# Schur and solve steps for two chunks at once, key, value and query products in one-bank halves, and another rule for the order of the steps

## Reference, cut to what matters

```python
def step(S, qkv):                       # scanned over the 8 chunks of a batch, for each head
    Qc, Kc, Vc = qkv                    # 128 x 64 each
    G = Kc.T @ Kc + 1e-4 * I
    W = jnp.linalg.solve(G, Kc.T @ Vc)
    U = I[:, :8]
    for _ in range(2):
        U, _ = jnp.linalg.qr(W @ U)
    Wr = U @ (U.T @ W)
    S_new = 0.9 * S + Wr
    return S_new, 0.125 * (Qc @ S_new)
```

## Time and profile before

| | |
|---|---|
| median of 3 runs | 1141.81 us (1141.43 to 1143.41) |
| the profiled execution | 1141.08 us |
| its span in the trace | 1139.3 us |
| busy: PE, DVE, ACT, POOL | 976.5, 650.0, 536.2, 196.8 us |
| mean granted clock of TensorE | 0.916 of 2.4 GHz |
| DMA | 117.49 MB, mean 103 GB/s |

### The profile page before, as it was taken

One profiled execution on the slowest core, in us unless ns is written; L12 is line 12 of the kernel. 1 busy time (PEld: TensorE's weight loads), 2 busy tenths in 40 slices (PEclk: granted clock), 3 DMA queues, 4 the chain that ended last, 5 costly groups with the idle time before them and its releaser, 6 DMA issues.

```text
span 1139.3 us, 41225 instructions
## 1 busy us (share of the span) xinstructions
PE 976.5 (86%) x18210; PEld 732.9 (64%) x18210; DVE 650.0 (57%) x1439; ACT 536.2 (47%) x1064; POOL 196.8 (17%) x246
## 2 busy tenths in 40 slices
PE   4898898996889986567988899899578989999997
PEld 2454445653545555446877788687456878888886
DVE  5772980999669995153675676588321243333333
ACT  2653334633544554342545544356444544444445
POOL 3431000010020001000122132221000232222223
PEclk9999999998999996677998999899656999999999
DMA  9543126634664576443144321423444121111100
GB/s 289 165 142 93 56 88 155 168 120 109 169 170 96 155 187 183 101 109 88 51 139 126 98 66 41 118 64 93 133 101 103 56 53 40 40 41 40 40 20 20
DMA packets 210912, 117.49 MB, mean 103 GB/s; under 512 B 145776, under 2 KB 197360, under 8 KB 209712
## 3 DMA queue, kind: packets, MB, share of 16 engines
q1 hardware_dynamic: 205264, 93.62, 31.3%
q0 software_dynamic: 5472, 21.24, 6.1%
HBM read 61.74 MB, written 53.08 MB: 101 GB/s over the span
## 4 chain that ended last, share of the span: by engine, by line
PE 73%; DMA 7%; ACT 7%; issue 5%; SPq 4%; DVE 4%; POOL 1%; POOLq 0%; DVEq 0%; ACTq 0%
PE psum L1107 19%; PE psum L1295 10%; PE psum L1117 9%; PE psum L1127 5%; PE psum L1328 5%; PE psum L1318 5%; PE psum L1214 3%; PE psum L1284 3%; DMA cu<-gc_d 3%; DMA schur_mem<-lead_d 2%; PE psum L1271 2%; PE psum L1200 2%; PE psum L1180 2%; ACT kv L740 2%; PE psum L1155 2%
## 5 line engine op out<-in xcount | busy, mean ns | idle before, releaser
L1107 PE MATMUL psum<-wqkv,xhat 128*128 128x512 f32 x512 | 241.0, 621 | 2.5 <-ACT xhat L732 2.3
L968 DVE SCALAR_TENSOR_TENSOR outer<-sweep_mem,rd 128x992 f32<-128x992 f32 (+30 forms) x248 | 187.4, 755 | 8.7
L974 DVE TENSOR_TENSOR sweep_mem<-sweep_mem,outer 128x992 f32<-128x992 f32 (+30 forms) x248 | 177.7, 716 | 8.5
L1107 PEld LDWEIGHTS psum<-wqkv,xhat 128*128 128x128 f32 x512 | 97.2, 197 | 115.5 <-issue 112.8
L740 ACT COPY kv<-psum 128x1024 f32<-128x1024 f32 x64 | 64.8, 1012 | 164.7 <-PE psum L1107 164.7
L1295 PE MATMUL psum<-wo,kv 128*128 128x256 f32 x512 | 124.4, 398 | 0.7 <-DVE state L1027 0.4
L1117 PE MATMUL psum<-xhat,wqkv 128*128 128x128 f32 x1024 | 124.6, 281 | 0.3 <-ACT nz L829 0.3
L669 POOL TENSOR_TENSOR hsplit<-gc,hsplit 128x512 f16<-128x512 f32 x64 | 74.6, 1166 | 284.9 <-ACT hsplit L860 284.8
L1117 PEld LDWEIGHTS psum<-xhat,wqkv 128*128 128x128 f32 x1024 | 120.6, 197 | 2.0 <-ACT nz L829 0.4
L1295 PEld LDWEIGHTS psum<-wo,kv 128*128 128x128 f32 x512 | 98.5, 197 | 16.1 <-DVE state L1027 0.6
L855 ACT ACTIVATE gc<-psum,b1c,alpha 128x128 f32<-128x128 f32 x256 | 96.8, 468 | 19.1 <-PE psum L1318 19.1
(11 more groups left out here) (117 smaller groups left out, 1389.0 us busy)
## 6 DMA issues: line engine op xcount, KB each, us to landing
gc_d<-gc SPq DMA_DIRECT2D x32, 512.0 KB, 3.4
schur_mem<-gc_d SPq DMA_DIRECT2D x32, 384.0 KB, 3.9
f_d<-fac SPq DMA_DIRECT2D x32, 272.0 KB, 2.2
fl<-f_d SPq DMA_DIRECT2D x32, 272.0 KB, 2.9
sv_d<-sv SPq DMA_DIRECT2D x32, 192.0 KB, 2.8
lead_d<-sweep_mem POOLq DMA_DIRECT2D x4, 1024.0 KB, 5.1
schur_mem<-lead_d SPq DMA_DIRECT2D x64, 64.0 KB, 3.7
r_d<-pt SPq DMA_DIRECT2D x32, 128.0 KB, 2.0
```

The source lines that it names most:

```text
L968: V.scalar_tensor_tensor(out=tile, in0=a[:, t, t + 1:HALF].unsqueeze(2).broadcast_to([P, m, HALF]), scalar=rd[:, t:t + 1], in1=a[:, t, t + ...
L974: V.tensor_tensor(rest, rest, tile, ALU.subtract).then_inc(swept, 1)
L1107: ins = mm(dst[:, cols], xnt[:, c, t], wqkv[:, n, t, cols], start=t == 0, stop=t == KT - 1)
```

## The change

`side()` is now called after every host step and tries one Schur step and one solve step. Both chains work on a pair of chunks (`e`, chunks 2e and 2e + 1), one pair at a time; a step is put only when the plan takes its predecessor's drain or load to be done (`ready`). `K`, `V` and `Q` become `KA`, `KB`, `VA`, `VB`, `QA`, `QB` of one bank and one ACT copy each. `WRA` and `WRB` of a turn come behind `QA` and `QB` of that same turn (one turn of the loop earlier). The plan's weights are new, DVE may be 1.2 us behind PE when a pivot is put, and banks are chosen by another key. The alternate buffers now hold the two chunks of a pair, so all but `gct` (still two pairs) are single for a pair. `NZ`'s results are read with another index (`2 * b + n`), with the same instructions.

```diff
-SIDE_EVERY = 1.7
+DVE_BEHIND = 1.2
-            if start > now["pe"]:
+            if start > now["pe"] + DVE_BEHIND:
                 return
+    def ready(step, c):
+        return max([0.0] + [at.get(e, 1e9) for e in follows(step, c)])
+    def bank(n):
+        def key(k):
+            t = max(free[k:k + n])
+            beside = max(free[k ^ 1], now["pe"]) if n == 1 else 0.0
+            return max(t, now["pe"]), -beside, k
+        return min(range(0, NBANKS, n), key=key)
...
-    def schur_slot():
...
+    def load_schur():
+        e = chain["schur_next"]
+        if e < NCH // 2 and at.get(("swept", 0, e // half_batch), 1e9) <= now["pe"]:
+            put("LC", e)
+            chain["schur"] += [("SP", e), ("SX", e), ("SV", e)]
+            chain["schur_next"] += 1
+    def schur_step():
+        if not chain["schur"]:
+            load_schur()
+        if not chain["schur"] or ready(*chain["schur"][0]) > now["pe"]:
+            return False
+        step, e = chain["schur"].pop(0)
+        put(step, e)
+        if step == "SP":
+            load_schur()
+        elif step == "SV" and e % half_batch == half_batch - 1:
+            open_at[1, e // half_batch] = at["SV", e] + 4.0
+        return True
+    def load_solve():
+        e = chain["solve_next"]
+        if e < NCH // 2 and at.get(("swept", 1, e // half_batch), 1e9) <= now["pe"]:
+            put("LS", e)
+            chain["solve"] += [("S", e), ("U", e), ("W", 2 * e), ("W", 2 * e + 1), ("Y", e), ("YT", e), ("Z", e)]
+            chain["solve_next"] += 1
+    def solve_step():        # as schur_step; the two W are put together, then load_solve(); after the batch's last Z, MLOAD
...
     def side():
-        return schur_slot() or solve_slot()
+        done = [schur_step(), solve_step()]
+        return any(done)
     def host(step, c):
         put(step, c)
-        main[0] += PE_WEIGHT.get(step, 0.0)
-        if main[0] >= SIDE_EVERY:
-            main[0] = 0.0
-            side()
+        side()
...
-        for step, at in (("K", c), ("V", c), ("T", c + 1), ("G", c)):
+        for step, e in (("KA", c), ("KB", c), ("VA", c), ("VB", c), ("T", c + 1), ("G", c)):
...
-        if on(r + 1):
-            put("WRA", r + 1)
-            put("WRB", r + 1)
...
         if on(r + 2):
-            host("Q", r + 2)
+            host("QA", r + 2)
+            host("QB", r + 2)
+            put("WRA", r + 2)
         if on(r):
             host("Y3", r)
+        if on(r + 2):
+            put("WRB", r + 2)
```

SP's load of a pair for the solve steps, and an ACT drain and a matmul step as examples of the rest:

```diff
-            def load_solve(c):
+            def load_solve(e):
...
-                if c >= 2:
-                    sp.wait_ge(*is_filled("U", c - 2))
+                if e:
+                    sp.wait_ge(*is_filled("U", e - 1))
+                for i in range(2):
+                    sp.dma_start(lps[:, i], comp_d[b].rearrange("(s c q) t n -> c (q t) s n", c=CPB, q=QUADS)[c % CPB + i]
+                                 ).then_inc(solve_loaded, 16)
+                    sp.dma_start(vv[:, i], sv_d[c + i][:, :, HALF:]).then_inc(solve_loaded, 16)
-                if c >= 2:
-                    sp.wait_ge(*is_filled("W", c - 2))
+                if e:
+                    sp.wait_ge(*is_filled("W", c - 1))
...
+                for a in range(2):
+                    for u in range(2):
+                        sp.dma_start(cu[rows(2 * a), u], src[rows(2 * a), u, :, :, HD:P]).then_inc(solve_loaded, 16)
...
+            def lower_rows(e):
+                act.wait_ge(*is_filled("U", e))
+                if e:
+                    act.wait_ge(*is_filled("W", 2 * e - 1))
                 for a in range(2):
                     sl = rows(2 * a + 1)
-                    ins = nc.scalar.copy(cu[sl, c % 2].rearrange("p (s u) n -> p u s n", u=2), src[sl])
-                ins.then_inc(drain("U", c), 1)
+                    ins = nc.scalar.copy(cu[sl].rearrange("p u c s n -> p (u c s n)"), place("U", e)[sl])
+                ins.then_inc(drain("U", e), 1)
...
             def gram(c):
                 dst = begin("G", c)
-                pe.wait_ge(*is_drained("K", c))
-                pe.wait_ge(*is_drained("V", c))
-                for h in range(PAIRS):
+                for half in range(2):
+                    pe.wait_ge(*is_drained(("KA", "KB")[half], c))
+                    pe.wait_ge(*is_drained(("VA", "VB")[half], c))
+                    for h in range(4 * half, 4 * half + 4):
```

More of the change, by code:

```diff
@@ new lines, in load_solve @@
+    def load_solve():
[5 more added lines that the diff above has]
+    def solve_step():
+        if not chain["solve"]:
+            load_solve()
+        if not chain["solve"] or ready(*chain["solve"][0]) > now["pe"]:
+            return False
+        step, e = chain["solve"].pop(0)
+        put(step, e)
+        if step == "W":
+            if e % 2 == 0:
+                put(*chain["solve"].pop(0))
+            load_solve()
+        elif step == "Z" and e % half_batch == half_batch - 1:
+            put("MLOAD", e // half_batch)
+            small_at[e // half_batch] = now["pe"] + 7.0
@@ L227, in load_factors @@
     def load_factors(r):
-        if 0 <= r < turns and r not in factors and ("Z", TURNS[r]) in where:
+        if 0 <= r < turns and r not in factors and ("Z", TURNS[r] // 2) in where:
             put("LF", r)
@@ new lines, in comp_inverse @@
+            def comp_inverse(e):
+                dst = begin("S", e)
+                pe.wait_ge(solve_loaded, 160 * (e + 1))
+                for c in range(2):
+                    for s in range(PAIRS // 2):
+                        at = HALF * (PAIRS // 2 * c + s)
+                        for q in range(QUADS):
+                            sl = rows(q)
+                            ins = mm(dst[sl, at:at + HALF], lps[sl, c, s, HALF:], lps[sl, c, s, 0:HALF], start=True, stop=True)
+                ins.then_inc(fill("S", e), 1)
@@ new lines, in lower_rows @@
+            def lower_rows(e):
+                dst = begin("U", e)
+                pe.wait_ge(*is_drained("S", e))
+                for c in range(2):
+                    for s in range(PAIRS // 2):
+                        for q in range(QUADS):
+                            at = BANK * (q % 2) + HD * (PAIRS // 2 * c + s)
+                            ins = mm(dst[rows(q | 1), at:at + HD], st[rows(q), c, s], vv[rows(q), c, s], start=True, stop=True)
+                ins.then_inc(fill("U", e), 1)
```

494 lines of the change are left out of this document (230 added, 264 removed).

## The result

The changed kernel takes 1045.3 us (median of 4 runs, 1041.37 to 1051.75) against 1141.62 (4 runs, 1139.5 to 1143.41): ratio 0.916, 95% interval 0.911 to 0.922. It is 96 us faster where 153 were forecast. The time lies in the range (950 to 1050) and near its slow end; it is outside the likeliest case's own range (955 to 1015). The profiled execution took 1048.18 us with a span of 1046.3 and a clock of 0.949.

What follows compares the result with a forecast made beforehand. PE bounds the kernel, busy 86% of the span, with two stretches of side steps only (174.5 us). Terms 413 + 5 + 295.5 + 3 + 282 = 998.5, less 12 for loads, give 986.5, so 988 us; range 950 to 1050.

Steps and rivals of the forecast that it cites:

- the likeliest case: Both stretches without host steps, before the first turn and before batch 2, all but closed: 955 to 1015 us, chance 0.62.
- loads covered: DMA waits for S and SP outside the two stretches, about 23 us: host steps between load and use take 12 off.
- Four pairs after a load of 6 us: 293 + 6 + 88 = 387: Batch 0's solve chain in the first stage: sweep 3 ends at 293, load 6 us, four pairs of 22 us.
- batch 0 can be there at 411: Batch 0's inverses before the first turn: small inverse and its way back add 24 us to the solve chain's end at 387.
- Rival 1: Solve loads late: all 16 pairs wait on PE, up to 59 us where 33 is paid now; 1014 us, chance 0.10.
- Part 1: Halves of K, V, Q: G's 17.8 us wait for V's copy goes (10 to 17.8), for 18 us of hidden ACT time.
- Part 2: WRA and WRB one turn earlier, no longer in front of WO: 13 us gained, bounds 0 and 18.
- Part 3, first stage: More side calls: first stage ends at 413 with 4 further solve chunks; wait before first turn falls from 101.5 to 5 us.
- Part 3, turns: Turns up to batch 2 take 295.5 us with 16 solve, 12 Schur chunks; sweeps take 80 us, batch 2 there at 681.
- The wait of 73 us goes to 0: PE's stretch without host steps before batch 2: batch 2 there at 681, before 713.5; 3 us left in the sum.
- rival 3: Batch 0 late, at 483: readiness test passes a pair only in 40 us; 70 us of waiting, about 1055 us, chance 0.07.
- rivals 1 and 2: First: late solve loads, 1014 us, chance 0.10. Second: sweeps among turns stay at 116 us, batch 2 late, about 1030, chance 0.13.

Runs made afterwards that it cites:

- parts 1 and 2 alone: The kernel before with halves of K, V, Q and WRA and WRB one turn earlier, old side slots kept: 1120.09 us, ratio 0.985.
- batch 2 held: The changed kernel with the solve chain tried first and Schur steps of batches 2 and 3 held until batch 0's last Z is put: 1035.25 us, ratio 0.908.
- the combined kernel: The changed kernel with batch 2 held and batch 0's small inverse moved behind the last pivot of sweep 5: 1030.72 us, ratio 0.906.

## Why the prediction was right in sign and short in size

The stretches, forecast and found:

| part of the sum | forecast | found | off |
|---|---|---|---|
| first stage, to last G | 413 | 429.1 | + 16 |
| wait before the first turn | 5 | 34.6 | + 30 |
| turns up to batch 2, with its wait | 298.5 | 314.3 | + 16 |
| rest | 282 | 268.3 | - 14 |
| loads covered | - 12 | in the parts above | + 12 |
| span | 986.5 | 1046.3 | + 60 |

**The step that failed** is "Four pairs after a load of 6 us: 293 + 6 + 88 = 387", with what is built on it, "batch 0 can be there at 411". The first NZ was possible at 463.7. By its terms: sweep 3 ended at 302.1 and not 293 (+ 9; the sweep before it started at 192.8 after 196.5, only 4 us earlier), from there to the first S were 27.4 us and not 6 (+ 21), the four pairs took 329.5 to 431.0 = 101.5 and not 88 (+ 14), and from Z to the first NZ went 32.7 and not 24 (+ 9). The biggest of these was readable before: the path from sweep 3 to the first S was 35.5 us in the kernel before (305.9 to 341.4). The 6 us is the constant that the plan uses for it, and I took the plan's figure where the trace had one. The Trainium skill (DMA: Bandwidth & Descriptors, Rules for kernel authors) wants a DMA issued early; the rows above show that here the issue itself was late, for 12 us behind a store in the same queue. Rival 1 looked for this loss 16 times over, as a wait of PE on each load (up to 59 us, found 1.6); it came once, on the path, and no row of PE's waits shows it, because PE did host work meanwhile.

**Part 1** was right in its mechanism (17.8 us of waits gone, and ACT's price as reckoned: 556.0 us busy with parts 1 and 2 alone after 536.2, + 20 where 18 was counted; in the changed kernel the drains of a pair save more than that, 531.4) and too small for this kernel, by what the halves do for the side steps: some 33 us by the run with whole K, V and Q.

**Part 2** was put at 13, between 0 and 18; measured some 7 to 10 by ratios, with intervals that overlap or nearly touch.

**Part 3, first stage.** The + 16 has two halves. PE's idle time in it fell from 52.1 to 43.3, by 9, where 17.8 was counted; new waits of small steps took the rest. And its busy time rose by 19.4 instead of 12.4. I had kept "no extra" for the clock, with the argument that the small matmuls now lie between long ones. They do, and the clock is still lower: 0.95 in the first stage, against 0.98. The window of the changed kernel in which the side steps are thickest, and PE's timeline around its start:

```profile
391.00:408.00 17.00, 15.07 (x362) 10.04 (x362) 15.75 (x37) 5.82 (x11) 0.00 (x0) 0.63 0.44 124
```

```profile
385.30 1.88 PE L1134 MATMUL psum<-wqkv,xhat 128*128 128x512 f32 x4
391.16 2.10 PE L1186 MATMUL psum<-schur_mem 32*32 32x32 f32 x64 [3.99 <-DMA schur_mem<-lead_d]
...
394.31 3.14 PE L1134 MATMUL psum<-wqkv,xhat 128*128 128x512 f32 x4
```

PE is busy for 15.07 of 17 us there, and the clock is 0.63. But the window begins behind a wait: PE stood idle for 3.99 us for the load of a Schur pair, and in it the clock fell to 0.50 (at 390). It rose, and fell again at 400, when PE had stood idle once more, for 1.8 us. At the low level the long products are slow as well, four in 3.14 us where they took 1.88 just before, and small steps directly behind long ones have the full clock: 64 matmuls of 32 x 32 take 1.20 us at 429.0. In the first stages of this kernel and of the one before, each of the ten falls of the clock comes in or directly behind an idle time of PE, of 1.3 to 7.6 us. So the small matmuls by themselves are not what lowers the clock here; the falls go with the waits that the side steps bring. With batches 2 and 3 held back these waits are gone from the end of the stage. The same window of the changed kernel and of the one with batch 2 held:

```profile
330.00:402.00 72.00, 64.15 (x1589) 40.44 (x1578) 67.67 (x127) 36.05 (x60) 0.84 (x3) 0.94 0.58 143
```

```profile
330.00:402.00 72.00, 68.72 (x1668) 42.43 (x1667) 67.71 (x126) 41.41 (x66) 0.85 (x3) 1.00 0.45 121
```

The clock is 1.00 instead of 0.94, PE is busy 4.6 us longer, and the last G comes at 409.1 (402.6 to 411.2 in the four kernels that hold batch 2). So part of the extra time is the price of Schur work that was put there before it was needed: its waits, and the clock that they cost.

**Part 3, turns.** "The wait of 73 us goes to 0" is right: 0, not even the 3 I left. But sweep 6 could not start at 403 as the sum has it; it is batch 3's first sweep and needs the last G. It started at 457.0, behind the small inverse of batch 0. The 80 us for a sweep among the turns held for the sixth (79.9) and not for the seventh (107.4), so that sweep 7 ended at 644.2, not 563. Batch 2 came in time all the same, the loads of its inverses issued by 773.7 and used by NZ at 789.1 with no wait, so at most 15 us of the forecast's margin of 32 are left. How thin that is the experiments show: two small edits of the order (the load planned 8 us earlier, DVE not allowed behind) bring the stretch back with 42 and 50 us. The turns up to batch 2 took 39 us more than before, where 27 less 6.5 was forecast, plus 3 for a wait. The matmuls in the windows say why: these turns held 7 to 8 solve chunks before, not the 10 that the sum starts from, and hold 18 to 20 now, not 16; the Schur chunks stayed 8 and did not become 12 (4 lie in the wait of 34.6 us). PE's busy time there rose by 35 us and its idle time by 4. The rest is 14 shorter than forecast because it holds 4 to 6 solve chunks and not 8, and because PE's idle time in it fell by 10 (18.7 to 9.0).

**Loads.** Outside the two stretches the kernel before has 23.2 us of DMA waits for S and SP, of which 12 were taken off. The changed kernel has 15.1 there, so 8 are gone; those of SP in the first stage stayed (11.0 and 10.9).

**By the signs that were named beforehand:** sweep 4 starts directly behind 3 (304.4 after 302.1), G waits for no copy, the clock is above 0.94. PE's idle time is 101 and not below 90, the last G at 429 and not 411, the first NZ at 463.7 and not before 430, and one stretch of more than 20 us is left. The last one, with NZ after 450 and PE waiting, is the sign of rival 3, batch 0 late, to which I gave 0.07. It held, with another cause (not the plan's test in each pair, but the path into the first) and with half its price: a wait of 34.6 us, not 70.

**Luck in the range.** The likeliest case did not come, and the time lies in the stated range only because that had been widened for rivals 1 and 2, neither of which came; the case that did, a late batch 0, was left out of it at 1055 and came at a smaller price. The direction and the mechanism of the gain (both stretches shrink as the chains end earlier) were right.

**What stays open:** how much of the 34.6 us can be had. The rows of the two paths say that a load stands 12 us behind a store before the first S, and in the combined kernel some 20 us before the first NZ; a kernel with both loads put ahead was not run. The only run that touched the first of them moved the planned time, and with it the whole order. And why the same list parts in time behind chunk 15, by up to 9 us at the last G, was not found; the clock that falls in waits of unequal length is in it, what starts it is open.

## What to carry to other kernels

When a chain of small steps is laid between host steps, read the whole way from one link to the next in the trace, queue by queue: an in-order queue can hold a ready load behind a store that waits for another engine, and no row of the bound engine's waits will show it. Never take a delay from the planner's own constants where the trace has the same stretch. A wait that is closed by the order alone has no margin until it is measured: move one constant of the plan and see whether it opens again.

## What the runs showed of the hardware

- The granted clock falls while PE waits, and the work behind the wait pays for it. In the changed kernel it fell to 0.50 in a wait of 3.99 us (387 to 391); the four 128 x 512 products behind it took 3.14 us instead of 1.88, and 64 matmuls of 32 x 32 took 2.10 us where at full clock they take 1.20 (429.0). Small matmuls directly behind long ones ran at full clock.
- Long products put between such steps raise the clock of the stretch (0.59 to 0.78), and 64 matmuls of 32 x 32 behind them take 1.20 instead of 1.92 us. It made the kernel slower all the same, by some 12 us in the traces and 17 by the ratios.
- Issuing a load costs SP real time: ten DMAs of a solve load from 318.68 to 325.4, 0.67 us each, and the four of a Schur pair 3.97 us (430.58 to 434.55), with everything behind them in the queue as late.
- The store of the factors of the last pair of batch 0, issued at 434.6 behind those loads, took 6.2 us to land, where the median of the 16 such stores is 3.7.
